# A graph network's edge loads laid out for 2 KB runs: attributes of four steps and first destinations, one core of Trainium2

## The reference

```
cat = concat([h[src], h[dst], edge_features])
m   = relu(cat @ W1 + b1) @ W2 + b2
agg = segment_sum(m, dst)
h   = gru_cell(agg, h)
```

## Time and profile before

| | |
|---|---|
| Median of 3 executions | 7556.06 us (7550.07 to 7564.09) |
| The profiled execution | 7545.64 us, its span 7543.9 us |
| Mean granted TensorE clock | 0.604 of full speed |
| Instructions | 30,852 |
| DMA, mean over the span | 43 GB/s, 322.65 MB in 430,799 packets |

### The profile page before, as it was taken

One profiled execution on the slowest core, in us unless ns is written; L12 is line 12 of the kernel. 1 busy time (PEld: TensorE's weight loads), 2 busy tenths in 40 slices (PEclk: granted clock), 3 DMA queues, 4 the chain that ended last, 5 costly groups with the idle time before them and its releaser, 6 DMA issues.

```text
span 7543.9 us, 30852 instructions
## 1 busy us (share of the span) xinstructions
PE 2731.1 (36%) x6948; PEld 1494.9 (20%) x6948; DVE 3484.9 (46%) x4568; ACT 341.4 (5%) x526; POOL 4766.7 (63%) x5016
## 2 busy tenths in 40 slices
PE   3343433343334323333333323332433333333334
PEld 2121222221122211111111111121211111111112
DVE  3444544454454434444444434443544444444445
ACT  1000000000000000000000000000000000000001
POOL 5666666666666466666666666656666666666664
PEclk6565566655665656566665666655666656566556
DMA  4222222222222112222222212212222222222221
GB/s 122 39 42 41 41 42 41 41 42 41 42 41 41 37 36 42 42 41 42 42 42 42 42 38 43 42 38 40 43 42 41 40 41 41 41 42 41 41 42 30
DMA packets 430799, 322.65 MB, mean 43 GB/s; under 512 B 89356, under 2 KB 349663, under 8 KB 430181
## 3 DMA queue, kind: packets, MB, share of 16 engines
q0 software_dynamic: 160224, 164.84, 14.1%
q1 hardware_dynamic: 212875, 116.67, 5.5%
q10 hardware_dynamic: 57506, 39.08, 1.9%
HBM read 297.33 MB, written 22.83 MB: 42 GB/s over the span
## 4 chain that ended last, share of the span: by engine, by line
another core or an unknown queue 37%; DVE 34%; issue 20%; PE 7%; DMA 1%; POOL 0%; ACT 0%; DVEq 0%; ACTq 0%; SPq 0%
DVE work_ps L1290 8%; DVE folds L1295 6%; DVE work_ps L1279 5%; DVE p_src L1276 5%; DVE sums L1305 2%; PE work_ps L772 2%; PE bank L785 1%; DVE hot L1250 1%; PE bank L773 1%; PE bank L804 1%; DVE pick L1261 1%; PE bank L805 1%; DVE n_hi L1319 1%; DVE bank L1325 1%
## 5 line engine op out<-in xcount | busy, mean ns | idle before, releaser
L634 POOL DMA_INDIRECT p_src<-p_tab,idx_all x4983 | 4740.9, 951 | 2719.3 <-issue 1538.3
L785 PE MATMUL bank<-hot,folds 128*128 128x96 f32 x2496 | 629.8, 398 | 2901.5 <-DVE folds L1295 1962.8
L785 PEld LDWEIGHTS bank<-hot,folds 128*128 128x128 f32 x2496 | 504.5, 281 | 3162.8 <-DVE folds L1295 2080.9
L772 PE MATMUL work_ps<-w_edges,msg 128*128 128x512 f32 x1248 | 1081.9, 965 | 68.1 <-DMA windows_sb<-q_tab 68.1
L1305 DVE TENSOR_TENSOR sums<-bank,sums 128x96 f32 x624 | 159.6, 256 | 1788.4 <-remote 1490.8
L1276 DVE TENSOR_TENSOR p_src<-work_ps,p_src 128x512 f32<-128x512 f32 x624 | 428.1, 686 | 1172.9 <-remote 772.7
L1279 DVE TENSOR_TENSOR work_ps<-p_src,bank 128x1024 f32<-128x1024 f32 x624 | 766.8, 1229 | 21.4
L1295 DVE TENSOR_REDUCE folds<-work_ps 128x256 f32<-128x1024 f32 x624 | 762.1, 1221 | 10.8
L1290 DVE SCALAR_TENSOR_TENSOR work_ps<-work_ps,rel 128x1024 f32<-128x1024 f32 x624 | 763.1, 1223 | 0.2
L782 PE MATMUL bank<-hot,counts 128*34 128x96 bf16 x416 | 66.3, 252 | 1158.9 <-DVE folds L1295 793.3
L1303 DVE TENSOR_TENSOR state<-bank,state 2x96 f32 x208 | 52.2, 251 | 871.1 <-remote 645.7
(11 more groups left out here) (150 smaller groups left out, 1434.3 us busy)
## 6 DMA issues: line engine op xcount, KB each, us to landing
p_src<-p_tab,idx_all POOLq DMA_INDIRECT x4983
msg<-in_edge_k SPq DMA_DIRECT2D x156, 256.0 KB
pick<-rel_tab SPq DMA_DIRECT2D x312, 124.0 KB
windows_sb<-q_tab ACTq DMA_DIRECT2D x312, 31.0 KB
pick<-q_tab ACTq DMA_DIRECT2D x312, 31.0 KB
windows_sb<-q_tab SPq DMA_DIRECT2D x312, 31.0 KB
pick<-q_tab SPq DMA_DIRECT2D x312, 31.0 KB
p_tab<-stage ACTq DMA_DIRECT2D x52, 117.0 KB
```

Of the source, the lines that this page charges most:

```text
L634: pool.indirect_dma_start(out=p_src[r][0:rows, t, :], out_offset=None, in_=p_tab[l][0:NODES, :], in_offset=bass.IndirectOffsetOnAxis(ap=id ...
L772: nc.tensor.matmul(edge_ps[k % 2], attrs[n % 2][:, s, :], w1_edges[:, l, :], start=True, stop=True)
L785: last = nc.tensor.matmul(fold_ps, folds[:, b, :], hot_all[n % 2][:, s * BLOCKS + b, 1:WINDOW + 1], start=(b == 0), stop=(b == BLOCKS - 1))
```

## The change

Three arrays get another layout. `edge_k` holds, for each group, 128 rows (one per partition) in which the four steps' 128 values stand side by side, so that a partition's data for a group is one run of 2 KB. `rel_tab` gets one row per block, in which all steps stand side by side, so that a group's values for a block are one run of 2 KB; it is stored with two DMAs instead of one. A second copy of the attributes in the old layout, `edge_s`, is handed in for the branch that isn't executed. Destinations in SBUF, bytes, semaphores and the number of DMAs per group are as before.

```diff
-        rel_tab = nc.dram_tensor("rel_tab", [STEPS // 2, 2 * BLOCKS * 128], F32).ap()
+        rel_tab = nc.dram_tensor("rel_tab", [BLOCKS, STEPS * 128], F32).ap()
...
-            sp.dma_start(rel_tab, first_rel).then_inc(rel_stored, 16)
+            for b in range(BLOCKS):
+                sp.dma_start(rel_tab[b].rearrange("(r s p) -> r s p", s=2, p=128),
+                             first_rel.rearrange("r (s b p) -> r s b p", s=2, b=BLOCKS)[:, :, b]).then_inc(rel_stored, 16)
...
-            sp.wait_ge(rel_stored, 16)
+            sp.wait_ge(rel_stored, 16 * BLOCKS)
...
-                sp.dma_start(attrs[n % 2], io["edge_k"][GROUP * g:GROUP * (g + 1)].rearrange("s q p -> q s p")).then_inc(edges_in[n % 2], 16)
-                wide = GROUP * BLOCKS * 128
-                row = rel_tab.rearrange("p e -> (p e)")[wide * g:wide * (g + 1)].rearrange("(s b p) -> b s p", b=BLOCKS, p=128)
+                sp.dma_start(attrs[n % 2], io["edge_k"][g].rearrange("q (s p) -> q s p", p=128)).then_inc(edges_in[n % 2], 16)
+                wide = GROUP * 128
                 for b in range(BLOCKS):
-                    sp.dma_start(hot_rows[n % 2][REACH * b:REACH * (b + 1), :].rearrange("n (s p) -> n s p", p=128),
-                                 row[b:b + 1].to_broadcast([REACH, GROUP, 128])).then_inc(rows_in[n % 2], 16)
+                    sp.dma_start(hot_rows[n % 2][REACH * b:REACH * (b + 1), :],
+                                 rel_tab[b:b + 1, wide * g:wide * (g + 1)].to_broadcast([REACH, wide])).then_inc(rows_in[n % 2], 16)
...
-        "edge_k": edge.transpose(0, 1, 3, 4, 2).reshape(STEPS, EDGE_TILES * EDGE_DIM, 128),
+        "edge_k": edge.transpose(0, 1, 3, 4, 2).reshape(GROUPS, GROUP, EDGE_TILES * EDGE_DIM, 128).transpose(0, 2, 1, 3).reshape(GROUPS, EDGE_TILES * EDGE_DIM, GROUP * 128),
+        "edge_s": edge.transpose(0, 1, 3, 4, 2).reshape(STEPS, EDGE_TILES * EDGE_DIM, 128),
```

More of the change, by code:

```diff
@@ L475, in front @@
                 sp.dma_start(pick[s][WINDOW + 1:KEDGE, :].rearrange("f (t p) -> f t p", p=128),
-                             io["edge_k"][bass.ds(m, 1)].rearrange("o (t f) p -> f (o t) p", f=EDGE_DIM)).then_inc(edge_in[s], 16)
+                             io["edge_s"][bass.ds(m, 1)].rearrange("o (t f) p -> f (o t) p", f=EDGE_DIM)).then_inc(edge_in[s], 16)
                 base = sp.value_load(base_i[0:1, bass.ds(m, 1)], min_val=0, max_val=NODES)
```

## The result

The changed kernel takes 7570.58 us (median of 20 executions, 7540.95 to 7599.43), the kernel before beside it 7548.16 us (20 executions, 7526.51 to 7577.27). The ratio is 1.0027 with a 95% interval of 1.0015 to 1.0038: slower by about 20 us, where 0.6% faster was forecast.

A forecast was written before the change was run, and what follows sets the result against it. It took TensorE's late signals to VectorE while GpSimd gathers as the bound. The start's -2 us and the swings' -44 us gave 7500 us against the profiled execution, 7510 us against the runs' median; range 7390 to 7590 us.

The forecast's parts named there:

- The bound: In the loop, TensorE's signals reach VectorE late while GpSimd gathers, and GpSimd then stops, 1026.6 us in 144 waits.
- Packets: On queue q1, attributes and rows go from 1008 to 252 packets a group, leaving 95,251 of 212,875.
- Time of the DMA engines: A 2 KB packet on q1 takes about 110 ns, a tenth less than the four it replaces (125 ns).
- SyncE's issue: SyncE issues the rows in about 1 us and four windows in 2 to 4 us; worth nothing on the path.
- The start: Before the first `mix`, SyncE is held up less by pieces of these loads: -2 us, bounds 0 and 15.6 us.
- The swings: In the loop, fewer packets cut short some late-signal waits of `keep`: -44 us, bounds 0 and 872 us.
- The third case: Slower: unbraked SyncE windows and longer packets delay gathers in the loop; 78 us at 0.5 us a group; chance 0.23.

The follow-up runs named there:

- e5: The kernel before, unchanged, as a control in a late series: 7545.4 us beside 7549.4 us, ratio 1.0002.
- e12: The changed kernel, unchanged, against the kernel before in a prompt series: 6423.7 us beside 6422.8 us, ratio 1.0001.
- e2: The kernel before with only the attributes in the new layout, plus their second copy, late series: 7641.7 us beside 7632.9 us, ratio 1.002.
- e3: The kernel before with only the first destinations (`rel_tab`, its stores and loads) in the new layout, late series: 7601.6 us beside 7632.9 us, ratio 0.9975.
- e13: The changed kernel with SyncE waiting for the rows to land before issuing windows, against the kernel before, prompt series: 6420.1 us beside 6420.4 us, ratio 1.0.
- e9: The kernel before plus a one-element memset on GpSimd ahead of each step's eight gathers, prompt series: 6423.3 us beside 6422.8 us, ratio 1.0.
- e10: The kernel before with the two loads of first destinations issued a second time per group into an unused tile, prompt series: 6437.7 us beside 6422.8 us, ratio 1.0023.
- e4: The kernel before loading, from the third group on, only one of four steps' attributes and first destinations, late series: 7599.1 us beside 7632.9 us, ratio 0.9961.
- e8: The changed kernel without the second copy of the attributes, against the kernel before, late series: 7563.8 us beside 7549.4 us, ratio 1.0024.
- e6: The changed kernel, unchanged, against the kernel before in a late series: 7560.0 us beside 7549.4 us, ratio 1.0016.
- e7: The kernel before with only the first destinations in the new layout, as e3, in another late series: 7571.2 us beside 7549.4 us, ratio 1.0024.
- e14: The changed kernel, unchanged, against the kernel before in a prompt series: 6421.5 us beside 6420.4 us, ratio 1.0002.
- e16: The kernel before with only the first destinations in the new layout, as e3, prompt series: 6420.5 us beside 6420.4 us, ratio 1.0.
- e18: The changed kernel, unchanged, against the kernel before in a prompt series: 6421.8 us beside 6420.9 us, ratio 1.0001.

## Why the prediction was wrong, by its own steps

*The bound.* Right for that execution: late signals and GpSimd's stops. What it couldn't know is that the same kernel takes 6420 us in other series; one chip showed both. Of the 1126 us between 7549 and 6423 us, 1104 lie in the idle time ahead of the gathers (2725.7 us in e5, 1621.8 us in e12), and they go together with the late signals.

*Packets.* Right: 95,251 worked out, 95,264 counted.

*Time of the DMA engines.* Right in the mean: about 110 ns taken, 109.6 ns by the page and 102.8 ns by the packets of the trace. But it is a mean of two: the attributes' pieces cost as much as the four that they replace (116.7 ns, e2), and all of the saving is the rows' (91.3 ns, e3). The Trainium skill's rule of full rate from 512 B ("DMA: Bandwidth & Descriptors", "Specifications") would have both equal; the attributes agree, and for the rows the measurement decides.

*SyncE's issue.* Half right. The rows went to 0.63 us (about 1 expected), the four windows from 10.6 to 6.4 us at the median (2 to 4 expected). The number of pieces ahead is part of the brake, but not all of it: e13's windows go in 1.55 us only once the rows are through. And some groups need 13.3 us before as after, as SyncE itself is slow there.

*The start.* -2 us forecast. `mix` began 5.2 us sooner in the profile, 104.31 for 109.46, but none of it reached the end: GpSimd has slots left until about 120 us and isn't stopped by the first step. In e12 too `mix` begins sooner (106.01 us, 110.05 us in e9), and the time is that of before. In e10, where `mix` begins at 123 us, GpSimd is stopped and the whole gets longer. The term was given to the path where it lies beside it.

*The swings.* This is the step that failed. It took two waits, one near loads and one apart from them, for a rule, and gave the loads 44 us of the late signals; the prediction itself called this a choice. e4 takes three quarters of the loads away and the idle time ahead of `keep` stays within 1%. The time went up by about 20 us instead. In place of the step the runs show: the late signals come and go with something outside the kernel, and taking away three quarters of the loads doesn't touch them.

*The third case* had the sign of the first measurement. What it said of the gathers' transfers is seen: q0's share rises from 14.1% to 16.1%, and to 16.7% with the rows alone. What it said of SyncE unbraked came only in part: 6.4 us for four windows and not 2 to 4. Nor did its sign show, more idle time ahead of L1276. And in prompt series q0's share goes from 15.1% (e9) to 18.2% (e12) at the same time, since GpSimd's issue is the bound and the gathers' landing is beside it. So a longer packet of a gather costs nothing there. In which way the late kernel got slower no run shows, so that this case had the sign may be luck.

*What stays open.* In prompt series the change is worth 0 (1.0001, 1.0002 and 1.0001, each to about 0.1%). In late series the changed kernel is slower: 1.0027 and 1.0016 (0.9999 to 1.0033), and 1.0024 without the second copy (e8). The cause isn't shown. Of the 26 us between the two profiled spans 16 are gathers of 955 ns, which e9 shows with the old layout too; whether such executions fell on one kernel more often than on the other in the timed runs can't be seen. That e6, e7 and e8 all had 954 ns and e5 951 ns, in one series, speaks for a tie between the two, and e3, e12, e14, e16 and e18 (951 or 952 ns with the new rows) against it. With the rows alone two late series gave 0.9975 and 1.0024, with intervals that exclude each other, so the sign of an effect of this size depends on the series; the whole change wasn't timed in the series of 0.9975. Whether braking SyncE helps under late signals isn't known either, as both series with it were prompt.

Nor is it shown what makes TensorE's signals late. It isn't every signal: in the trace of before TensorE's `spread_step` starts 0.05 us after the fold that it waits for ends (3010.92 and 3010.87 us), while TensorE's own increments and SyncE's instructions crawl. Two rivals are untested. As all late series came first, it may be a matter of when, and not of the chip. And the recording of the profile may have a part: the late traces hold only 331 to 374 of the 624 increments of one semaphore (the folds'), the prompt ones all of them, and every execution timed here was recorded.

## What to carry to other kernels

Work out what the whole of a transfer is worth before its layout: here leaving out three quarters of the loads gave 0.39% in a late series, and doubling half of them in prompt ones cost 0.23%, most of it at the start. A load that is asked for one group ahead, and for which nobody waits in the trace, has little to give by the way its pieces are cut: nothing in the prompt series here. And where a profile's largest waits have no named releaser, don't hang a term on them from two examples: time the unchanged kernel several times on several chips first, as it may turn out that the waits aren't the kernel's own.

## What the hardware showed that was not expected

- The same program takes 7549 us (7522.67 to 7571.55) in one series and 6420 us (6417.47 to 6424.67) in a later one, on the same chip. In the first its executions scatter over 0.6%, in the second over 0.1%. In the first, 1808.9 us of idle time stand ahead of L1305 (e5); in the second 5.2 us in the changed kernel (e14).
- While signals are late, an increment of TensorE is acted upon 12 to 33 us after its matmul: in the trace of before VectorE starts L1305 at 3007.47 us and L1276 at 3019.33 us after matmuls that ended at 2984.8 and 2986.1 us, and ScalarE starts at 2996.17 us after one that ended at 2984.4 us. GpSimd's gathers keep to 1.256 us from one to the next meanwhile.
- In the late series SyncE's register moves, 29 ns at the median, take up to 1.4 us; in the prompt ones 43 ns at most.
- A gather's issue takes 951 ns in most executions and 954 to 956 ns in others, all through the execution, with the old layout as with the new; over 4983 of them that is up to 18 us.
- A 2 KB piece takes 116.7 ns in a 128-partition load (e2) and 91.3 ns in the loads that copy one row to 62 partitions (e3). The latter lengthen the gathers' packets by a seventh to a fifth: q0's share goes from 14.1% to 16.1%, and in later series from 12.6% (e5) to 15.0% (e6) and from 15.1% (e9) to 18.2% (e12).
- A one-element memset on GpSimd between two gathers is free in a prompt series (e9): it takes 89 ns and fits in the 0.3 us gap.
